# Nine block sums of a graph network on one Trainium2 core: gathered source rows and 32-wide one-hots in place of dense counts

## The chip, the cores and the metric

The kernel runs on one core of one Trainium2 chip. The metric is the device time of one execution in microseconds. The kernel before takes 1509.97 us (median of 3 runs, 1509.72 to 1510.40).

## What is computed

A graph of N = 6250 nodes has 206,250 edges (`src`, `dst`), sorted by `dst`. The input is normalised row by row and cut at zero; three layers follow, and the log-softmax of the last is added to the input:

```
def _mean_agg(x, src, dst, n):
    msg_sum = segment_sum(x[src], dst, num_segments=n)
    cnt = segment_sum(ones((src.shape[0], 1)), dst, num_segments=n)
    return msg_sum / maximum(cnt, 1.0)

def _sage_conv(x, src, dst, Wl, bl, Wr):
    return _mean_agg(x, src, dst, x.shape[0]) @ Wl.T + bl + x @ Wr.T

h = relu(layernorm(x))
h = relu(batch_norm(_sage_conv(h, ..., Wl0, bl0, Wr0)))   # 128 -> 256 features
h = relu(batch_norm(_sage_conv(h, ..., Wl1, bl1, Wr1)))   # 256 -> 256
h = _sage_conv(h, ..., Wl2, bl2, Wr2)                     # 256 -> 128
return x + log_softmax(h)
```

The edges are data: the program finds them on the chip. A flag says whether the quick way has found all of them; if not, a general and slow way (`general`) runs, which it does not do here.

## The kernel before

**Dense counts.** The destinations are cut into NB = 25 blocks of BD = 250 nodes, the sources into NA = 49 tiles of 128. For each block layer 0 builds a matrix C with one row per source and one column per destination; an entry is the number of edges between the two. A block's sum over its edges is then a product of features and C: 49 tiles, each feature matrix in two float16 parts (high and low), so 98 matmuls of 250 columns (`pe_agg`, L802). Layer 1 has 256 features and so 196 matmuls a block. Layer 2 first multiplies with its weights, which leaves 128 features and 98 matmuls. C is stored in DRAM (`C_dram`, 3.06 MB a block) while layer 0 runs and loaded again, half a block at a time, in layers 1 and 2 (`block_load`, L1160).

**Layer 0** runs over phases c = 0 to NB of NST = 13 steps each; step i of phase c counts ten of the 125 destination pairs of block c and adds a thirteenth of block c - 1's sum. Its parts in order of a block's way:
- ScalarE and VectorE find where the block's edges begin; GpSimd gathers a row of destinations (`pool_rows`, L331) and windows of 128 edges for each pair of destinations (`pool_windows`, L342). This is done for four blocks at once, in chores that `chores` puts at fixed steps. GpSimd, VectorE and TensorE turn the windows into a table (`pool_place`, L351 and L353; `dve_table`; `pe_turn`, L779).
- VectorE makes one-hots of source and position with `dve_hot` (L621), two operations for every two steps, in three buffers.
- TensorE multiplies them (`pe_cells`, L795, 10 matmuls of 98 columns a step) into four banks used in turn; ScalarE copies these as float16 into `ring` (L459).
- TensorE adds up the block before (`pe_agg`), VectorE divides by the degree (`dve_mean`, L630), TensorE multiplies with the weights (`pe_linear`, L810 and L813), ScalarE adds the bias, VectorE takes the statistics for the batch normalisation.

Layer 1 ends only when its statistics are in; so does layer 0.

**Layers 1 and 2** begin with a prelude: the features are normalised and turned (`pe_pair`, L1226) or multiplied (`pe_quad`, L1237), ScalarE and VectorE write the two parts, and TensorE adds up the first two blocks in between (their C is still in `ring`). Then come the other 23 blocks (`pe_layer1`, `pe_layer2`), each with the products of one finished block inside.

The order on each engine is the order of the Python code for it; engines meet at semaphores. Of the DMA queues, SP's carries loads, stores and C, GpSimd's the gathers only. GpSimd has nothing to do after layer 0's last table.

Steps and orders are set by these lines:

```
orders = [list(range(NB)), list(range(NB))[::-1], list(range(NB))]
...
for c in range(NB + 1):
    work = [(a, part) for a in range(NA) for part in range(2)]
    for i in range(NST):
        t = NST * c + i
        if c < NB:
            pe_cells(c, i)
        ...
        upto = len(work) * (i + 1) // NST
```

Of the kernel before, what the change touches and what calls it, by code (L numbers as in the profile page):

```python
# [6 lines left out]
F32 = mybir.dt.float32  # L7
F16 = mybir.dt.float16
# [5 lines left out]
P = 128  # L14
# [11 lines left out]
NTAB = 8  # L26

# [12 lines left out]
def gnn_program(nc, n_edges, x, pairs, dst_rows, samples, const_f, iota_h, WlT, WrT, vecs, out):  # L40
# [10 lines left out]
    assert N % BD == 0 and NW <= P and GPK * NW <= 512 and NT * P <= EP and NB >= 4  # L51
# [4 lines left out]

    batches = [(0, 1)]
    while batches[-1][1] < NB:
        batches.append((batches[-1][1], min(NB, batches[-1][1] + NBT)))
# [60 lines left out]
    def bank_before(t, h):  # L120

        t -= 2
        while t >= 0 and h >= banks_of(t):
            t -= 2
        return banks_upto(t) - banks_of(t) + h + 1 if t >= 0 else 0
# [3 lines left out]
    visit = {lc: v for v, lc in enumerate(visits)}  # L129
# [9 lines left out]
    nquad = -(-NA // 4)  # L139

    with ExitStack() as ctx:
# [49 lines left out]
        tot = sb("tot", [P, NB + 1])  # L191
# [19 lines left out]
        early = upper if NA * 128 >= need else sb("early", [P, need])  # L211
        win = early[:, 0:NBT * 256].bitcast(I32).rearrange("p (w n two) -> p w n two", w=NBT, two=2)
        wrk = early[:, NBT * 256:NBT * (256 + 3 * P)].rearrange("p (k n e) -> p k n e", k=3, e=P)
        hots = sb("hots", [P, NHOT - 1, HOT], F16)
        hot = [early[:, NBT * (256 + 3 * P):need].bitcast(F16)] + [hots[:, k, :] for k in range(NHOT - 1)]
        tab = sb("tab", [P, NTAB, 2, P], F16)
# [12 lines left out]
        def hot_pos(h):  # L229
            return hot[h % NHOT][:, 0:GPH * NW].rearrange("p (q x t) -> p q x t", x=NW, t=2)  # L230


# [7 lines left out]
        d_out = [sem(f"d_out{s}") for s in range(4)]  # L240

# [8 lines left out]
                             "v_z2", "v_dd", "v_fin", "v_own"))  # L250

        a_sample, a_inrow, a_degree, a_tab, a_cells, a_lnstd, a_relu, a_hi0, a_h0 = (
# [8 lines left out]
        n_set = GD + 1 + 5  # L261
# [10 lines left out]
        def lin_bank1(c):  # L272
            return [7, 2][c % 2]
# [23 lines left out]
        def sync_layer0():  # L297
# [14 lines left out]
            for c in range(NB + 1):  # L312
                if c >= 1:
                    rcb_load(c - 1)
# [4 lines left out]
                if c < NB:  # L319
                    sp.wait_ge(a_cells, banks_upto(NST * c + NST - 1))  # L320
                    sp.dma_start(C_dram[c, :, :], ring[:, c % 2, :]).then_inc(d_store[c % 2], 16)

# [37 lines left out]

        def pool_layer0():
# [7 lines left out]
            pool.memset(zeros_h[:, :], 0.0).then_inc(p_set, 1)  # L369
            pool_rows(0)  # L370
            pool_windows(0)
            pool_rows(1)
            pool_windows(1)
            for t in range(NST * NB):
# [7 lines left out]
                if t in ln_at and ln_at[t] in act_groups:  # L382
                    pool_lo(ln_at[t])

# [1170 lines left out]
```

## Time and profile before

| | |
|---|---|
| median of 3 runs | 1509.97 us |
| the profiled execution, its time | 1508.48 us |
| its span in the profile | 1506.7 us |
| TensorE matmul, busy | 1418.1 us, 94% |
| VectorE | 616.1 us, 41% |
| ScalarE | 544.1 us, 36% |
| GpSimd | 120.0 us, 8% |
| granted TensorE clock, mean | 0.993 |
| chain that ended last: TensorE, VectorE, ScalarE | 80%, 10%, 5% |
| layer 0 | from 0 to 550 us |
| layer 1 | 550 to 1177 us |
| layer 2 | 1177 us to the end |

The busy time of an engine is an average over three layers of different kinds, so what an edit is worth is read in its own layer. The chain that ended last is followed back from the last instruction: its shares tell which work the time hangs on. Times of the trace below count from the start of the span. Where a row of the timeline merges instructions (x4), its duration is that of all of them.

### The profile page before, as it was taken

To read this page: it belongs to the slowest core of one execution; us is meant where nothing else is said; L and a number is where in the kernel's file an instruction comes from. 1 tells how busy PE (TensorE), PEld (TensorE's weight loads), DVE (VectorE), ACT (ScalarE), POOL (GpSimd) and SP (SyncE) were. 2 spreads that over 40 slices of the span, in tenths; PEclk is the share of its full clock that TensorE was granted. 3 is DMA by queue.
4 is the path that set the end of the run, shared out by engine and by line. 5 is a ranking of instruction groups with operands and counts; after the bars stand their busy time and mean duration, and the time that the engine had idled before them with its cause. 6 is when DMAs were issued, how large, how long until landed. Compare 5 with 4: busy or idle time off the path is not lost.

```text
span 1506.7 us, 31846 instructions
## 1 busy us (share of the span) xinstructions
PE 1418.1 (94%) x14074; PEld 1280.7 (85%) x14074; DVE 616.1 (41%) x954; ACT 544.1 (36%) x1298; POOL 120.0 (8%) x81
## 2 busy tenths in 40 slices
PE   1499999999999989999999999999999899999997
PEld 1388898988898979899999999999999898888886
DVE  6998898989898943100000000000000222112212
ACT  4897979897878747100000000000000430000001
POOL 2323131313130000000000000000000000000000
PEclk9999999999999999999999999999999999999999
DMA  5244454545454422434343333334340358888882
GB/s 165 88 165 157 158 189 189 189 183 195 180 198 175 176 95 86 140 128 160 122 151 130 132 130 132 130 132 141 126 161 10 93 223 305 285 302 289 300 286 99
DMA packets 49914, 252.24 MB, mean 167 GB/s; under 512 B 7790, under 2 KB 31532, under 8 KB 34796
## 3 DMA queue, kind: packets, MB, share of 16 engines
q1 hardware_dynamic: 47372, 243.59, 45.4%
q0 software_dynamic: 2400, 6.56, 1.5%
q8 instruction: 114, 1.87, 0.5%
q14 instruction: 28, 0.23, 0.0%
HBM read 168.50 MB, written 81.62 MB: 166 GB/s over the span
## 4 chain that ended last, share of the span: by engine, by line
PE 80%; DVE 10%; ACT 5%; issue 3%; DMA 2%; POOL 1%; DVEq 0%; SPq 0%; POOLq 0%; ACTq 0%
PE bank L802 62%; PE bank L795 6%; DVE hots L621 5%; PE bank L810 4%; PE bank L813 4%; ACT ring L459 2%; DVE parts L621 2%; PE bank L1237 2%; PE bank L1439 1%; DMA parts<-in_pairs_dram,first_i 1%; ACT junk L412 1%; PE bank L1226 1%; POOL parts L351 0%; PE bank L1450 0%; ACT Z L436 0%
## 5 line engine op out<-in xcount | busy, mean ns | idle before, releaser
L802 PE MATMUL bank<-ring,parts 128*128 128x250 f16 x9800 | 1121.3, 270 | 1.3 <-DVE agm L630 1.1
L802 PEld LDWEIGHTS bank<-ring,parts 128*128 128x128 f16 x9800 | 937.6, 97 | 100.9 <-issue 1.6
L459 ACT CAST ring<-bank 128x490 f16<-128x490 f32 x625 | 322.8, 587 | 81.6 <-PE bank L795 79.1
L621 DVE TENSOR_TENSOR hots<-iotas,tab 128x2560 f16<-128x2560 f16 (+1 forms) x232 | 277.3, 1245 | 1.5 <-ACT tab L420 0.8
L1277 ACT ACTIVATE Z<-bank,vec 128x250 f32<-128x250 f32 x48 | 19.9, 466 | 529.5 <-PE bank L813 529.5
L630 DVE SCALAR_TENSOR_TENSOR agm<-bank,bnw,rcb 128x250 f32<-128x250 f32 x50 | 21.5, 473 | 375.4 <-PE bank L802 375.4
L795 PE MATMUL bank<-hots 128*128 128x98 f16 x2080 | 136.7, 212 | 33.3 <-DVE hots L621 30.8
L795 PEld LDWEIGHTS bank<-hots 128*128 128x128 f16 x2080 | 120.3, 99 | 47.1 <-DVE hots L621 36.4
L621 DVE TENSOR_TENSOR parts<-iotas,tab 128x2560 f16<-128x2560 f16 (+1 forms) x118 | 139.4, 1222 | 2.2 <-ACT tab L420 1.2
L1397 ACT ACTIVATE junk<-rows_i 128x128 f32<-128x128 f32 (+1 forms) x49 | 14.7, 301 | 253.0 <-DVE rows_i L1426 253.0
L693 DVE BATCH_NORM_STATS2 st<-Z 128x6 f32<-128x250 f32 x96 | 35.2, 408 | 152.8 <-ACT Z L1277 152.3
L630 DVE SCALAR_TENSOR_TENSOR agm<-bank,isp,rcb 128x250 f32<-128x250 f32 x25 | 11.9, 477 | 166.8 <-PE bank L802 166.8
L795 PE MATMUL bank<-parts 128*128 128x98 f16 x1045 | 69.0, 212 | 11.5 <-DVE parts L621 10.2
L795 PEld LDWEIGHTS bank<-parts 128*128 128x128 f16 x1045 | 60.2, 99 | 19.8 <-DVE parts L621 14.2
L810 PE MATMUL bank<-Z,wr 128*128 128x250 f32 x288 | 76.5, 374 | 0.0
L813 PE MATMUL bank<-agm,wl 128*128 128x250 f32 x288 | 76.5, 374 | 0.0
L813 PEld LDWEIGHTS bank<-agm,wl 128*128 128x128 f32 x288 | 54.8, 190 | 6.0
L331 POOL DMA_INDIRECT rows_i<-in_dst_rows_dram,row_i x25 | 41.5, 1661 | 191.7 <-DVE row_i L508 185.9
L1213 DVE TENSOR_TENSOR parts<-bank,parts 128x512 f16<-128x512 f32 (+2 forms) x38 | 25.6, 674 | 73.8 <-ACT parts L1207 73.8
L810 PEld LDWEIGHTS bank<-Z,wr 128*128 128x128 f32 x288 | 50.8, 190 | 4.6
L342 POOL DMA_INDIRECT parts<-in_pairs_dram,first_i x25 | 41.4, 1655 | 64.4 <-DVE first_i L515 58.9
L1191 ACT ACTIVATE Z<-Z,bnw 128x256 f32<-128x256 f32 (+2 forms) x76 | 45.9, 655 | 1.6 <-DVE bnw L1180 1.6
(118 smaller groups left out, 541.3 us busy)
## 6 DMA issues: line engine op xcount, KB each, us to landing
c_blocks<-ring SPq DMA_DIRECT2D x25, 3062.5 KB, 10.6
ring<-c_blocks SPq DMA_DIRECT2D x46, 1562.5 KB, 6.5
ring<-c_blocks SPq DMA_DIRECT2D x46, 1500.0 KB, 6.6
rcb<-rc_row SPq DMA_DIRECT2D x75, 125.0 KB, 7.7
Z<-in_x_dram SPq DMA_DIRECT2D x4, 768.0 KB, 6.7
out_dram<-rows_i SPq DMA_DIRECT2D x24, 128.0 KB, 5.3
smp_i<-in_samples_dram SPq DMA_DIRECT2D x1, 403.0 KB, 3.3
rows_i<-in_dst_rows_dram,row_i POOLq DMA_INDIRECT x25, 4.0
```

The costliest lines, as they stand in the source:

```text
L331: pool.indirect_dma_start(out=rows_i[:, k, :], out_offset=None, in_=dst_rows, in_offset=bass.IndirectOffsetOnAxis(ap=row_i[:, c:c + 1], ax ...
L342: pool.indirect_dma_start(out=win[:, k, :, :].rearrange("p n two -> p (n two)"), out_offset=None, in_=flat_pairs, in_offset=bass.IndirectO ...
L459: act.copy(blk[c % 2][:, :, d0:d0 + GD * GPK].rearrange("p a (g d) -> p a g d", d=GD), bank[(0, 1, 5, 6)[(2 * t + h) % 4]][:, 0:GPK * NW] ...
L621: ins = dve.tensor_tensor(o[:, 0:q, :, :], iota2[:, 0:w, :].unsqueeze(1).to_broadcast((P, q, w, 2)), place.unsqueeze(2).to_broadcast((P, q ...
L630: ins = dve.scalar_tensor_tensor(agm[:, v % 2, m, :], bank[b][:, 0:BD], scale if isinstance(scale, float) else scale[:, m:m + 1], rcb[:, v ...
L693: dve.bn_stats(st[:, m, b, :], Z[:, m, BD * b:BD * b + BD]).then_inc(v_stats, 1)
L795: ins = pe.matmul(b[:, o:o + NW], bs[:, q0 + g // 2, :, g % 2], ps[:, q0 + g // 2, :, g % 2], start=True, stop=True)
L802: return pe.matmul(bank[b][:, 0:BD], view[0:r, a, part, m * P:m * P + P], blk[c % 2][0:r, a, :], start=(a, part) == (0, 0), stop=(a, part) ...
L810: pe.matmul(bank[b][:, BD * m:BD * m + BD], wr[layer][:, k, m * P:m * P + P], Z[:, k, BD * c:BD * c + BD], start=(k == 0), stop=False)
L813: ins = pe.matmul(bank[b][:, BD * m:BD * m + BD], wl[layer][:, k, m * P:m * P + P], agm[:, v % 2, k, :], start=False, stop=(k == nk - 1))
L1191: act.activation(Z[:, k, c0:c0 + w], Z[:, k, c0:c0 + w], ACT.Relu, bias=bnw[:, layer, 5, k:k + 1], scale=bnw[:, layer, 4, k:k + 1]).then_i ...
L1237: ins = pe.matmul(bank[t % 3][0:r, P * (a - 4 * t):P * (a - 4 * t) + P], Z[:, k, P * a:P * a + r], wl[2][:, k, :], start=(k == 0), stop=(k ...
```

## The change

Of the 25 blocks, blocks 20 to 23 become "loose". Blocks 22 and 23 are no longer counted densely at all, blocks 20 and 21 are, as the first two of the new order `seq` of ND = 23 counted blocks. In layer 0 the sums of blocks 20, 22 and 23 are gathered, in layer 1 those of all four, in layer 2 those of 22 and 23: nine block sums.

Such a sum works on half blocks of 125 destinations ("windows"), cut into four spans of 31, 31, 31 and 32 destinations. Each span's edges stand in 9 (the last: 10) tiles of 128 edges. For a tile GpSimd gathers the 128 source rows from a table of the features in DRAM, both parts side by side (`pool_round`, an indirect DMA of 128 rows of 512 bytes in layers 0 and 2, of 1024 in layer 1). TensorE multiplies them with the tile's one-hot, 128 edges by 32 destinations (`pe_round`); the four spans write partitions 0, 32, 64 and 96 of one bank. A round is one tile of each span: 9 rounds a window, the last with a fifth tile, 37 gathers and 37 matmuls. There are 6, 8 and 4 windows, so 54, 72 and 36 rounds, and two buffers for a round's rows. Then VectorE divides, TensorE turns the sum (`pe_group_turn`), ScalarE writes it where the products read it (`act_gmean`), and the block's products follow (`lin_at`). Rounds are placed evenly between the dense steps by `place`: in layer 0 one every 4.26 steps from step 39 on, in layer 1 one every 12.2 tiles, in layer 2 one every 25.4 tiles.

New besides: the features go to DRAM as a table once a layer (`table_store`, on SP's queue: 3.2, 6.4 and 3.2 MB), and in layer 2 both its halves stand ahead of the first block loads; VectorE makes a one-hot of 1280 elements a window (`dve_group_hot`); one gather, a few small operations and 20 transposes early in layer 0 find the edges of the spans; two windows of layer 0 are only counted, against a column of ones. Counts in layer 0 now use three banks instead of four. Layer 0 has 24 phases instead of 26, and its first sum starts in phase 2, not 1.

```diff
+    loose = [NB - 5, NB - 4, NB - 3, NB - 2]
+    gathered = [[loose[0], loose[2], loose[3]], loose, loose[2:]]
+    seq = loose[0:2] + list(range(NB - 5)) + [NB - 1]
+    ND = len(seq)
+    wins = [[2 * loose.index(b) + h for b in gathered[layer] for h in range(2)] for layer in range(3)]
+    rounds = [[(n, k, t) for n, k in enumerate(wins[layer]) for t in range(RPG)] for layer in range(3)]
+    def tiles_of(t):
+        return [(t, j) for j in range(4)] + ([(t + 1, 3)] if t == RPG - 1 else [])
...
-    orders = [list(range(NB)), list(range(NB))[::-1], list(range(NB))]
+    orders = [list(range(1, ND)), list(range(2, ND))[::-1], list(range(2, ND - 1)) + [0, 1, ND - 1]]
...
+    begin = [3 * NST, 14, 24]
+    spans = [NST * (ND - 1), NA * (len(orders[1]) - 2) - 12, NA * (len(orders[2]) - 2) - 40]
+    for layer in range(3):
+        nh = len(rounds[layer]) + 2 + (len(only_counted) if layer == 0 else 0)
+        place.append([begin[layer] + (spans[layer] - begin[layer]) * h // nh for h in range(nh)])
...
+        for r in range(len(rounds[layer])):
+            take[layer].setdefault(at[r], []).append(r)
+    for r in range(len(rounds[0])):
+        fetch.setdefault(place[0][r - 2] if r >= 2 else begin[0] - 8, []).append(r)
...
+        def pool_round(layer, r):
+            n, k, t = rounds[layer][r]
+            if r >= 2:
+                pool.wait_ge(t_round, rbase[layer] + r - 1)
...
+            for i, (tile, j) in enumerate(tiles_of(t)):
+                o = 40 * k + 4 * tile + j
+                pool.indirect_dma_start(
+                    out=got[layer][:, 5 * (r % 2) + i, 0:rowf[layer]], out_offset=None, in_=tables[layer],
+                    in_offset=bass.IndirectOffsetOnAxis(ap=src_i[:, o:o + 1], axis=0)).then_inc(d_got[r % 2], 16)
...
-                                     bank[(0, 1, 5, 6)[(2 * t + h) % 4]][:, 0:GPK * NW]
+                                     bank[(0, 1, 5)[(n - 1) % 3]][:, 0:GPK * NW]
...
+        def pe_round(layer, r):
+            if t == 0:
+                pe_sums_free(layer, n)
+                pe.wait_ge(v_ghot, wbase[layer] + n + 1)
+            pe.wait_ge(d_got[r % 2], landed[layer, r])
+            g = ghot(layer, n)
+            for i, (tile, j) in enumerate(tiles_of(t)):
+                ins = pe.matmul(b[32 * j:32 * j + 32, 0:w], g[:, 2 * tile + j // 2, :, j % 2],
+                                got[layer][:, 5 * (r % 2) + i, 0:w], start=(tile == 0), stop=(tile == WT[j] - 1))
+            ins.then_inc(t_round, 1)
...
         def sync_layer2():
+            for a0, a1 in ((0, FULL // 2), (FULL // 2, NA)):
+                table_here(a_hi2, v_lo2, 4, a1)
+                table_store(2, small, a0, a1)
             for k in range(2):
                 block_load(2, 2, k)
                 block_load(2, 3, k)
```

GpSimd's queue in layer 0. Before, after the low parts of the features (L358), it holds row and window gathers and the place computations alone:

```order
L358 TENSOR_TENSOR parts<-Z,parts 128x4x128 x8
L358 TENSOR_TENSOR parts<-Z,parts 106x128
L331 DMA rows_i<-in_dst_rows_dram,row_i 128x256 x4
L342 DMA parts<-in_pairs_dram,first_i 128x256 x4
L351 TENSOR_SCALAR parts<-parts 128x512
L353 TENSOR_TENSOR parts<-parts 128x512
```

The same queue with the change, from the first place computation on (`got_f` holds the gathered rows, `src_i` their numbers, `table` is the features' table in DRAM; L491, L493, L471 and L482 are the L351, L353, L331 and L342 of before):

```order
L491 TENSOR_SCALAR parts<-parts 128x512
L493 TENSOR_TENSOR parts<-parts 128x512
L513 DMA got_f<-table,src_i 128x256 x29
L471 DMA rows_i<-in_dst_rows_dram,row_i 128x256 x4
L513 DMA got_f<-table,src_i 128x256 x12
L482 DMA parts<-in_pairs_dram,first_i 128x256 x4
L513 DMA got_f<-table,src_i 128x256 x9
L491 TENSOR_SCALAR parts<-parts 128x512
L493 TENSOR_TENSOR parts<-parts 128x512
L513 DMA got_f<-table,src_i 128x256 x28
```

Where 8 gathers stood for four blocks, some 50 more now stand between them, and the window gathers that VectorE waits for are behind them.

TensorE's queue in layer 0 with the change, two rounds apart (L1128 counts, L1135 adds up the dense block, L1188 is `pe_round`):

```order
L1128 MATMUL bank<-parts 128x98 x10
L1135 MATMUL bank<-ring,parts 128x250 x7
L1128 MATMUL bank<-parts 128x98 x10
L1135 MATMUL bank<-ring,parts 128x250 x8
L1188 MATMUL bank<-got_f,parts 32x257 x4
L1128 MATMUL bank<-hots 128x98 x10
L1135 MATMUL bank<-ring,parts 128x250 x7
```

Before, such rows are the pairs of count and sum alone; every fourth or fifth pair is now followed by a round, which waits for its landing with all that stands behind it.

SP's queue at the start of layer 2 with the change (L409 loads degrees, L460 is `table_store`, L1584 `block_load`):

```order
L409 DMA rcb<-rc_row 128x250 [waits v_mean] x2
L460 DMA table<-parts 128x24x256 [waits v_lo2,a_hi2] x2
L460 DMA table<-parts 106x256
L1584 DMA ring<-c_blocks 128x6250 [waits t_half] x2
L1584 DMA ring<-c_blocks 128x6000 [waits t_agg] x2
```

The three L460 rows are new and stand between the degrees and the block loads, which followed each other before.

## Rows read from the trace of the kernel before

**Rows 1.** Table by stretches: us, then busy us (instructions) per engine, clock, DMA share, GB/s.
```profile
111.00:540.00 429.00, 415.14 (x5152) 377.06 (x5149) 390.48 (x464) 350.19 (x804) 90.43 (x46) 1.00 0.49 182
...
640.00:1160.00 520.00, 520.00 (x4519) 469.92 (x4517) 34.43 (x86) 18.26 (x44) 0.00 (x0) 1.00 0.37 130
...
1240.00:1490.00 250.00, 250.00 (x2244) 224.37 (x2243) 51.18 (x132) 19.77 (x110) 0.00 (x0) 1.00 0.83 285
```

**Rows 2.** Chain of waits, its longest pieces: start us, us, what.
```profile
348.32 8.06 DMA parts<-in_pairs_dram,first_i
...
644.47 20.97 PE bank L802 x196
668.83 20.98 PE bank L802 x196
```

**Rows 3.** Timeline of TensorE in layer 0: start us, us, engine line op, operands, count.
```profile
129.08 0.63 PE L795 MATMUL bank<-hots 128*128 128x98 f16 x10
129.55 1.02 PE L802 MATMUL bank<-ring,parts 128*128 128x250 f16 x8
130.41 0.63 PE L795 MATMUL bank<-parts 128*128 128x98 f16 x10
```

**Rows 4.** Timeline of GpSimd, with the idle time before in brackets.
```profile
32.40 0.95 POOL L342 DMA_INDIRECT parts<-in_pairs_dram,first_i  x1 [0.30 <-issue]
...
74.36 1.08 POOL L358 TENSOR_TENSOR parts<-Z,parts 106x128 f16<-106x128 f32 x1 [2.74 <-ACT parts L439]
...
174.75 2.08 POOL L331 DMA_INDIRECT rows_i<-in_dst_rows_dram,row_i  x1 [38.86 <-DVE row_i L508]
...
179.54 2.19 POOL L331 DMA_INDIRECT rows_i<-in_dst_rows_dram,row_i  x1 [0.31 <-issue]
182.03 0.96 POOL L331 DMA_INDIRECT rows_i<-in_dst_rows_dram,row_i  x1 [0.30 <-issue]
192.00 2.00 POOL L342 DMA_INDIRECT parts<-in_pairs_dram,first_i  x1 [9.02 <-DVE first_i L515]
...
207.77 1.92 POOL L351 TENSOR_SCALAR parts<-parts 128x512 f32<-128x512 f32 x1 [7.53 <-DVE parts L530]
209.78 2.17 POOL L353 TENSOR_TENSOR parts<-parts 128x512 f32<-128x512 f32 x1
...
270.33 1.98 POOL L342 DMA_INDIRECT parts<-in_pairs_dram,first_i  x1 [9.02 <-DVE first_i L515]
```

**Rows 5.** Timeline of TensorE in layer 1's prelude: four transposes.
```profile
559.38 0.60 PE L1226 MATMUL bank<-cf,Z 128*128 128x128 f32 x4
```

**Rows 6.** Timeline of VectorE beside the gathers of 174.75 to 182.99 us.
```profile
174.42 2.58 DVE L621 TENSOR_TENSOR parts<-iotas,tab 128x2560 f16<-128x2560 f16 x2
176.92 5.07 DVE L621 TENSOR_TENSOR hots<-iotas,tab 128x2560 f16<-128x2560 f16 x4
181.90 0.73 DVE L693 BATCH_NORM_STATS2 st<-Z 128x6 f32<-128x250 f32 x2
182.55 0.92 DVE L621 TENSOR_TENSOR parts<-iotas,tab 128x768 f16<-128x768 f16 x2
```

**Rows 7.** Line L342: landings of four gathers at 28.6 to 32.4, then at 192.0 to 199.3.
```profile
DMA to landing us min/median/max: 2.6/2.7/3.1
...
DMA to landing us min/median/max: 3.4/5.9/7.9
```

**Rows 8.** Timeline of TensorE at layer 0's end.
```profile
533.50 4.99 PE L802 MATMUL bank<-ring,parts 128*128 128x250 f16 x45
...
554.70 0.53 PE L1226 MATMUL bank<-cf,Z 128*128 128x128 f32 x2 [5.05 <-ACT Z L1191]
```

**Rows 9.** Timelines of SP and TensorE at layer 2's start; the page's row of block stores.
```profile
1209.49 18.69 SPq L1160 DMA_DIRECT2D ring<-c_blocks  x4
...
1228.01 2.95 PE L802 MATMUL bank<-ring,parts 128*128 128x250 f16 x26 [0.45 <-DVE agm L630]
...
c_blocks<-ring SPq DMA_DIRECT2D x25, 3062.5 KB, 10.6
```

More of the change, by code:

```diff
@@ L139, in gnn_program @@
     nquad = -(-NA // 4)
+    begin = [3 * NST, 14, 24]
+    spans = [NST * (ND - 1), NA * (len(orders[1]) - 2) - 12, NA * (len(orders[2]) - 2) - 40]
+    place = []
+    for layer in range(3):
+        nh = len(rounds[layer]) + 2 + (len(only_counted) if layer == 0 else 0)
+        place.append([begin[layer] + (spans[layer] - begin[layer]) * h // nh for h in range(nh)])
+    near = max(0, min(3, (spans[0] - begin[0]) // len(place[0]) - 1))
+    take, fold, turn_at, lin_at, only_at, hot_at = ([{} for _ in range(3)] for _ in range(6))
@@ new lines, in gnn_program @@
+    for layer in range(3):
+        at = place[layer]
+        for r in range(len(rounds[layer])):
+            take[layer].setdefault(at[r], []).append(r)
+        for n, k in enumerate(wins[layer]):
+            e = RPG * (n + 1)
+            fold[layer].setdefault(at[e - 1] + near, []).append(n)
+            turn_at[layer].setdefault(at[e], []).append(n)
+            if n % 2:
+                lin_at[layer].setdefault(at[e + 1], []).append(gathered[layer][n // 2])
+            hot_at[layer].setdefault(at[max(0, e - RPG - 2)], []).append(n)
@@ new lines, in pe_sums_free @@
+        def pe_sums_free(layer, n):
+            if layer == 0 and n > len(wins[0]):
+                pe.wait_ge(v_gcnt, n)
+            elif gbase[layer] + n:
+                pe.wait_ge(v_gsum, gbase[layer] + n)
+        def pe_round(layer, r):
+            n, k, t = rounds[layer][r]
+            b = bank[sum_bank[layer]]
+            w = 257 if layer == 0 else rowf[layer]
+            if t == 0:
[7 more added lines that the diff above has]
+            ins.then_inc(t_round, 1)
@@ new lines, in pe_only @@
+        def pe_only(n):
+            i = len(wins[0]) + n
+            pe_sums_free(0, i)
+            pe.wait_ge(v_ghot, i + 1)
+            pe.wait_ge(p_set, n_set)
+            g = ghot(0, i)
+            for t in range(RPG):
+                for tile, j in tiles_of(t):
+                    ins = pe.matmul(bank[6][32 * j:32 * j + 32, 256:257], g[:, 2 * tile + j // 2, :, j % 2], ones_h[:, 0:1],
+                                    start=(tile == 0), stop=(tile == WT[j] - 1))
+            ins.then_inc(t_only, 1)
@@ new lines, in pe_group_turn @@
+        def pe_group_turn(layer, n):
+            pe.wait_ge(v_gsum, gbase[layer] + n + 1)
+            if gbase[layer] + n:
+                pe.wait_ge(a_gmean, sum(len(wins[k]) * 2 * (rowf[k] // 256) for k in range(layer)) + 2 * n * (rowf[layer] // 256))
+            for m in range(rowf[layer] // 256):
+                o = turned_at[layer] + P * m
+                ins = pe.transpose(bank[turned_bank[layer]][:, o:o + P], gsum[layer][:, P * m:P * m + P], ident)
+            ins.then_inc(t_gturn, 1)
```

742 lines of the change are left out of this document (554 added, 188 removed).

## The prediction, before the changed kernel was run

> **What bounds the kernel now.** I read the table by stretches first, then the chain of waits, then the timelines of each engine. In layer 1 TensorE is busy for the whole 520.00 us of the stretch and VectorE for 34.43; in layer 2 the same, with the DMA engines at 0.83 of their time [rows 1]. The chain shows layer 1 as TensorE alone: 196 matmuls of a dense block in 20.97 us, 107 ns each, block after block 24.36 us apart, the rest being the products with the weights [rows 2]. So whatever leaves TensorE there is gained in full. Layer 0 is different. In its 429 us TensorE is busy 415, VectorE 390, ScalarE 350 [rows 1], and the chain passes through GpSimd's gathers of the edge windows, which take 8.06 us to land [rows 2]. A step (one of 13 of a block) costs TensorE 0.47 us of counting and 0.86 us or less of block sum [rows 3]; the real pace is read from two window gathers that lie four blocks, 52 steps, apart: 270.33 - 192.00 = 78.3 us, 1.51 us a step and 19.6 us a block [rows 4].
>
> **What goes.** Layer 1 loses four dense blocks: 4 x 20.97 = 83.9 us [rows 2]. Layer 2 loses two of 98 matmuls: 196 x 0.107 = 21.0 us. Layer 0 loses two of its 26 block phases (each 19.6 us, so 39 us) and the sums of one more block. The products with the weights all stay.
>
> **What comes on TensorE.** A half block needs 37 matmuls of 32 result rows, in four column strips, the longest strip ten deep. Layer 1 has 8 such windows of 512 columns, 296 matmuls; a matmul of 512 columns by the 107 ns of 250 is 219 ns [rows 2]. If the four strips run side by side, that is 80 x 0.219 = 17.5 us; if one after the other, 64.8. The trace of before has no matmul in a strip. I take 22, near the lower end, since the four write different partitions of one bank and no data of one feeds another. Layer 2: 148 matmuls of 256 columns, 4.4 to 16.3 us, taken as 5.5. The turns add 16 transposes in layer 1 and 4 in layer 2, at 0.15 us [rows 5]: 2.4 and 0.6 us.
>
> For strips only a page has a price. The Trainium skill (TensorE: Matmul & The Clock Gate, Part 3, Measured speedup vs the span model) gives 2.38 times for three column strips; by that, an estimate, the two layers would pay 27 + 7 us and the sum would be 6 us higher. No row here shows it.
>
> **What comes on GpSimd, and this decides.** 222 + 296 + 148 gathers of 128 rows. Their price is in the trace twice over. Where VectorE runs short work only, a gather, as the one at 32.40, is 0.95 us busy and 0.30 us behind the last: one in 1.26 us. In layer 0 they start 2.43 us apart on average, (182.03 - 174.75) / 3, and last 2.08 to 2.19 us [rows 4]. The difference is what VectorE does: one-hots back to back, each an operation with two SBUF inputs, 2.5 us a pair; and the fourth issue, again 0.96 us, fell just where a batch statistic ran instead [rows 6]. Each gather waits through two one-hots. Landing grows from 2.7 to 5.9 us at the median [rows 7]. So I price a gather at 1.26 us of VectorE's free time or 2.49 us of its one-hot time.
>
> A page goes further. The Trainium skill (SBUF — State Buffer, Who interferes with whom, and the warning on DMAs from GpSimd ahead of it) has an exclusive lock that blocks the other engine for a whole instruction, with a DMA going from about 620 to 3100 ns beside a copy. Five times 0.95 us would be an estimate of 4.75 us a gather, and the sum some 70 us higher; the rows agree with the lock, not with the factor.
>
> Layer 0, per round of 4.11 gathers, 54 rounds over the steps 31 to 264. GpSimd also has 36 of its old gathers there (0.67 a round) and five place computations of 1.92 + 2.17 us [rows 4] (0.38 us a round). VectorE's one-hot time is 6 pairs of 2.49 and one of 0.87 us a block [rows 6], 15.8 us, 18 blocks, so 5.3 us a round. In those 5.3 us GpSimd does 2.1 of its 4.78 gathers, the other 2.65 need 3.34 us free: the round takes 5.3 + 3.34 + 0.38 = 9.0 us. TensorE's own work between two takes is 4.26 steps x 1.51 = 6.4 us. GpSimd is slower, so TensorE stands at each take until the rows land, in order, with the counting and the dense sum behind it; VectorE then stops when its three one-hot buffers are full, which is where the free time comes from. The landing time itself is hidden, as two buffers of rows alternate. The first gather waits for the table in DRAM: the last low parts are made by 75.4 us [rows 4], and its 3.2 MB take like a block's store some 10.6 us [rows 9]; so 88 us. 88 + 54 x 9.0 = 574, + 3 to land = 577. Then 34 steps at 1.51 us and a last phase without counting, as before from about 535 to 549.7 [rows 8], 14 us: layer 0 ends at 643 instead of 549.7, **93 us later**. The 54 rounds' own matmuls (6 to 24 us) and the removed sums lie under GpSimd's time and count nothing; without that cover both would show. Three banks instead of four for the counts cost nothing for the same reason: ScalarE, which empties them, has 350 of 429 us busy and TensorE's stops give it more.
>
> Layers 1 and 2 are not held by GpSimd: one-hots are gone, a round is 4.11 x 1.26 = 5.2 us, and TensorE has 12.2 steps of 0.43 us plus products between takes, 6.2 us or more. At the starts something is late. In layer 1 the table's last quarter leaves SP only when the last parts are made; behind two half loads, then some 5.3 us to write (half a block's store), 5 to issue round 0, 3 to land, against some 13 us until the first take: 3 us. In layer 2 SP now issues both table halves, which wait for the last low parts, ahead of the first block loads. The four half loads took 18.69 us from 1209.49, 4.7 each, and TensorE wanted the first at 1228.01 [rows 9]. Started at about 1225 behind 1.6 MB, the first half lands near 1235 and the second near 1244: 11 us of waiting in all, between 0 if the loads catch up and 20.
>
> **The sum**, on the profiled execution's 1508.5 us: layer 0 +93; layer 1 -83.9 + 22 + 2.4 + 3 = -56.5; layer 2 -21.0 + 5.5 + 0.6 + 11 = -4. That is 1541; the median of the runs lies 1.5 above the profiled one, so **1542 us**.
>
> **Rivals.**
> A. The gathers keep the quiet 1.26 us in layer 0 too. Then GpSimd needs 4.78 x 1.26 + 0.38 = 6.4 us a round, just TensorE's own pace, and layer 0 gains: -39, about -5 for the third block's sum, +16 for matmuls of rounds no longer covered, -28 in all. Total 1510 - 28 - 60 = **1422 us**. For it: the quickest landing in layer 0's burst is 3.4 us after its issue, near the quiet 2.7 [rows 7]. Against: every burst in layer 0 has its first three issues at 2.0 to 2.2 us. 8%. A page points this way: the Trainium skill (DMA: Bandwidth & Descriptors, Anatomy of one DMA) calls the generation of descriptors small and most of the 2 us a receipt. The trace contradicts it, with 0.95 us on GpSimd for each even when quiet.
> B. The other sign by the same mechanism, only weaker: layer 0 loses less than the others gain. The other layers give 60.5 us; so the rounds must end 32 us sooner, a round of 8.4 us, which is a gather at 2.04 us in one-hot time. At 1.7 us a round takes 7.8, layer 0 is 26 us longer, and with strips fully side by side and no start waits (-75) the total is **1461 us**. For it: the 2.43 is from bursts of four, never from a stream. 10%.
> C. The strips run one after the other: +43 and +11 in layers 1 and 2, none in layer 0: **1596 us**. 12%.
> D. GpSimd's order hurts too: windows of the next blocks now stand behind gathers, VectorE waits for them before it makes one-hots, and gathers wait for TensorE's rounds. Each of five batches losing 8 us more, as one window's landing [rows 2]: **1582 us**. 15%.
> The forecast itself, contention at 2.2 to 2.8 us and strips mostly parallel: 55%.
>
> **Numbers.** Low end: a gather at 2.04 us (the point of B) with strips fully parallel and no start waits, 1495, and a little of B; high end: C with a round at 9.2 us, 1605. I give 1485 to 1605, which leaves out A, most of B and what lies beyond C and D together. A change of 0.2% (3 us) is about what can be measured. Faster over 0.2%: A and B and the low tail, 0.20; within: 0.02; slower: 0.78.
>
> **What would show it.** GpSimd gathers of about 2 us in layer 0 and 0.95 us later; TensorE's wait before the 257-column matmuls, released by the landing, near 2.5 us x 54; VectorE idle about a third between 100 and 580 us; layer 0's last matmul near 643 us. Layer 1 blocks still 24.4 us plus four rounds; four 512-column matmuls in about 0.3 us, not 0.88. Wrong if issues in layer 0 are 1.26 us apart, or TensorE's waits there are on one-hots, or the granted clock falls in the gaps and layer 0 becomes longer than GpSimd's time.

## The result and the profile after

The changed kernel takes **1622.24 us** (median of 4 runs, 1616.38 to 1636.87) against 1510.18 for the kernel before (median of 4, 1509.72 to 1511.29): ratio 1.0755, 95% interval 1.0684 to 1.0827. It is slower, as forecast, but by 112 us where 32 were forecast, and outside the range. The profiled execution took 1621.26 us, with a span of 1619.3.

The layers end where TensorE waits five microseconds for the normalised features. From the timeline of TensorE after the change, the first rows of layers 1 and 2, and the first row behind layer 2's prelude:

```profile
697.29 1.11 PE L1650 MATMUL bank<-cf,Z 128*128 128x128 f32 x4 [5.05 <-ACT Z L1615]
...
1284.27 1.01 PE L1661 MATMUL bank<-wl,Z 128*128 128x128 f32 x3 [5.24 <-ACT Z L1615]
...
1340.60 1.64 PE L1135 MATMUL bank<-ring,parts 128*128 128x250 f16 x7 [11.27 <-DMA ring<-c_blocks]
```

A layer's end is the start of that wait: 697.29 - 5.05 = 692.2, and 1279.0. Before, by the same rule, 549.7 [rows 8] and 1177.3.

| | before | after | difference | forecast |
|---|---|---|---|---|
| layer 0 | 549.7 | 692.2 | +142.5 | +93 |
| layer 1 | 627.6 | 586.8 | -40.8 | -56.5 |
| layer 2 to the end | 329.4 | 340.3 | +10.9 | -4 |

The table by stretches, the same stretches as [rows 1]:

```profile
111.00:540.00 429.00, 333.13 (x3611) 276.67 (x3608) 270.47 (x329) 247.04 (x565) 292.84 (x221) 0.88 0.45 151
640.00:1160.00 520.00, 505.94 (x4532) 433.12 (x4530) 96.05 (x211) 90.22 (x206) 233.30 (x244) 0.99 0.56 191
1240.00:1490.00 250.00, 230.83 (x2011) 200.82 (x2010) 47.96 (x109) 40.93 (x110) 93.73 (x99) 0.96 0.67 229
```

In layer 0 no engine is full. TensorE gets 3611 matmuls done in 429 us where it had 5152; by the busy time of one before (415.14 / 5152) they are 291 us of work. They took 333, and 33 of these 42 us lie in stretches at the lower clock: the granted clock fell to 0.88, with 18 stretches between 100 and 640 us, 123 us in all, at 1.2 GHz, where before there is one of 3.4 us, behind the layer's end. The other 96 us are waits. GpSimd is busy 293 of 429 us. Its gathers, and what they waited for, from the groups of instructions between 100 and 640 us:

```profile
L513 POOL DMA_INDIRECT got_f<-table,src_i x222 | 297.9, 1342 | 154.7 <-PE bank L1188 94.3 <-issue 57.2 <-remote 3.1
```

1.34 us on average, and a wait of 94 us for TensorE's rounds: GpSimd waits for TensorE far more than TensorE for it. TensorE's waits between 111 and 640 us, and ScalarE's (engine, tile and line, released by: us, times, longest). "Issue" stands where no wait is found that ended just then, "remote" where a signal came at a moment at which no recorded instruction ended:

```profile
PE bank L1128 <- ACT ring L632: 43.2, 40, 4.5
PE bank L1128 <- issue: 29.7, 18, 4.8
PE bank L1188 <- DMA got_f<-table,src_i: 17.1, 5, 9.7
PE bank L1128 <- DVE hots L830: 15.5, 4, 8.7
...
ACT ring L632 <- PE bank L1128: 154.9, 169, 5.7
ACT ring L632 <- remote: 45.6, 23, 5.2
```

TensorE's waits for gathered rows to land, the takes (L1188), cost 17 us, not 54 times 2.5. The counting (L1128) waits for ScalarE's copies, and ScalarE's copies (L632) wait for the counting. One such place, in the timeline of TensorE, then of ScalarE, VectorE and GpSimd:

```profile
218.22 0.40 PE L1128 MATMUL bank<-hots 128*128 128x98 f16 x5
221.66 0.59 PE L1128 MATMUL bank<-hots 128*128 128x98 f16 x5 [3.05 <-issue]
222.05 1.86 PE L1135 MATMUL bank<-ring,parts 128*128 128x250 f16 x8
223.71 0.61 PE L1128 MATMUL bank<-hots 128*128 128x98 f16 x5
228.85 0.59 PE L1128 MATMUL bank<-hots 128*128 128x98 f16 x5 [4.52 <-ACT ring L632]
```

```profile
222.49 0.57 ACT L632 CAST ring<-bank 128x490 f16<-128x490 f32 x1 [0.89 <-PE bank L1128]
228.22 1.04 ACT L632 CAST ring<-bank 128x490 f16<-128x490 f32 x2 [5.16 <-remote]
...
228.39 2.58 DVE L830 TENSOR_TENSOR hots<-iotas,tab 128x2560 f16<-128x2560 f16 x2 [10.01 <-remote]
...
221.66 0.95 POOL L513 DMA_INDIRECT got_f<-table,src_i  x1 [0.30 <-issue]
...
225.44 0.96 POOL L513 DMA_INDIRECT got_f<-table,src_i  x1 [0.30 <-issue]
```

Every copy empties the five matmuls of one bank, and all 575 copies and 2875 counting matmuls are in the trace, so they can be paired by number. The copy at 228.22 belongs to the matmuls at 218.22. ScalarE had been idle for 5 us, VectorE for 10, both on the same signal of TensorE, which the trace's semaphore record has at 228.20, 9.6 us behind the end of those matmuls; the next two banks' signals follow at 228.27 and 228.40, though their matmuls started 2 us apart. **TensorE's signals arrive late, in a bunch, while GpSimd issues gathers 1.26 us apart.** Counted over the layer from 100 us on: 69 of 514 copies begin more than 0.5 us after both their matmuls (by the trace's ends) and ScalarE's earlier work are over, 105 us together. Before it is 0 of 560. The record of signals says the same without any pairing: of the 626 of TensorE between 100 and 690 us, 131 come more than 0.5 us behind the end of the last matmul that could have sent them, before none of 682; those of ScalarE, VectorE and GpSimd are all within 0.02 us. The ends of matmuls are modelled in such a trace, so a late signal cannot be told from a matmul that ended late. With three banks between the two engines, TensorE then waits too. That reading needed experiments.

### The profile page after: what moved, and what is told of

Read it like the earlier page. It is cut to its first block, busy times and chain, and to the rows that moved or that the text cites. A ratio compares the mean times of both kernels' runs of the same rounds, so it can differ in the third digit from the quotient of the medians.

```text
span 1619.3 us, 31087 instructions
## 1 busy us (share of the span) xinstructions
PE 1398.3 (86%) x13334; PEld 1188.7 (73%) x13334; DVE 615.7 (38%) x1013; ACT 537.2 (33%) x1285; POOL 805.7 (50%) x746
## 4 chain that ended last, share of the span: by engine, by line
PE 70%; issue 7%; POOL 6%; ACT 5%; DMA 5%; DVE 5%; another core or an unknown queue 2%; SPq 0%; DVEq 0%; ACTq 0%; POOLq 0%
PE bank L1135 49%; PE bank L1128 7%; POOL got_f L513 4%; PE bank L1150 3%; PE bank L1153 3%; PE bank L1188 3%; ACT ring L632 3%; DMA got_f<-table,src_i 2%; DVE hots L830 2%; PE bank L1661 1%; DMA hots<-table,src_i 1%; PE bank L1935 1%; POOL hots L513 1%; PE bank L1650 1%
## 5 line engine op out<-in xcount | busy, mean ns | idle before, releaser
L1135 PE MATMUL bank<-ring,parts 128*128 128x250 f16 (+1 forms) x8526 | 1023.9, 274 | 14.9 <-DMA ring<-c_blocks 11.3
L1135 PEld LDWEIGHTS bank<-ring,parts 128*128 128x128 f16 (+1 forms) x8526 | 820.6, 99 | 133.0 <-issue 22.8
L513 POOL DMA_INDIRECT hots<-table,src_i x444 | 425.2, 958 | 528.3 <-DMA table<-parts 236.4
L632 ACT CAST ring<-bank 128x490 f16<-128x490 f32 x575 | 302.6, 579 | 242.4 <-PE bank L1128 175.8
L513 POOL DMA_INDIRECT got_f<-table,src_i x222 | 297.9, 1342 | 154.7 <-PE bank L1188 94.3
L830 DVE TENSOR_TENSOR hots<-iotas,tab 128x2560 f16<-128x2560 f16 (+1 forms) x214 | 253.1, 1230 | 52.3 <-PE bank L1128 31.3
L1128 PE MATMUL bank<-hots 128*128 128x98 f16 x1915 | 144.0, 223 | 94.3 <-ACT ring L632 42.2
L1128 PEld LDWEIGHTS bank<-hots 128*128 128x128 f16 x1915 | 117.8, 105 | 118.3 <-DVE hots L830 42.8
L830 DVE TENSOR_TENSOR parts<-iotas,tab 128x2560 f16<-128x2560 f16 (+1 forms) x108 | 128.0, 1227 | 23.2 <-PE bank L1128 21.6
L1128 PE MATMUL bank<-parts 128*128 128x98 f16 x960 | 72.2, 222 | 38.3 <-ACT ring L632 17.7
L1128 PEld LDWEIGHTS bank<-parts 128*128 128x128 f16 x960 | 58.8, 105 | 51.0 <-ACT ring L632 21.0
L1153 PE MATMUL bank<-agm,wl 128*128 128x250 f32 x256 | 69.3, 378 | 0.0
L1188 PE MATMUL bank<-hots 128*32 128x512 f16 (+1 forms) x444 | 41.7, 356 | 5.5 <-DMA hots<-table,src_i 5.5
```

The costliest lines, as they stand in the source:

```text
L513: pool.indirect_dma_start(out=got[layer][:, 5 * (r % 2) + i, 0:rowf[layer]], out_offset=None, in_=tables[layer], in_offset=bass.IndirectOf ...
L632: act.copy(blk[c % 2][:, :, d0:d0 + GD * GPK].rearrange("p a (g d) -> p a g d", d=GD), bank[(0, 1, 5)[(n - 1) % 3]][:, 0:GPK * NW] .rearra ...
L830: ins = dve.tensor_tensor(o[:, 0:q, :, :], iota2[:, 0:w, :].unsqueeze(1).to_broadcast((P, q, w, 2)), place.unsqueeze(2).to_broadcast((P, q ...
L1128: ins = pe.matmul(b[:, o:o + NW], bs[:, q0 + g // 2, :, g % 2], ps[:, q0 + g // 2, :, g % 2], start=True, stop=True)
L1135: return pe.matmul(bank[b][:, 0:BD], view[0:r, a, part, m * P:m * P + P], blk[c % 2][0:r, a, :], start=(a, part) == (0, 0), stop=(a, part) ...
L1153: ins = pe.matmul(bank[b][:, BD * m:BD * m + BD], wl[layer][:, k, m * P:m * P + P], mean[:, k, :], start=False, stop=(k == nk - 1))
```

## The experiments

My theories from this trace: **G**, the gathers that GpSimd issues hold up the others; **S**, the strip matmuls of the rounds do; **B**, three count banks instead of four. Layer ends below are read as above; "late copies" are those just counted (how many, and us together).

| run | layer 0 ends | layer 1 | layer 2 | time, us | late copies, us |
|---|---|---|---|---|---|
| before | 549.7 | 627.6 | 329.4 | 1510.2 | 0 |
| changed | 692.2 | 586.8 | 340.3 | 1622.2 | 69, 105 |
| no_gathers_l0 | 548.6 | 587.6 | 339.8 | 1477.8 | 2, 2 |
| three_banks_before | 554.6 | 629.1 | 329.4 | 1514.9 | 0 |
| whole_array_rounds | 693.3 | 615.3 | 344.6 | 1655.1 | 65, 99 |
| idle_gathers_before | 676.1 | 628.8 | 329.1 | 1636.0 | 57, 93 |
| idle_loads_sp | 556.7 | 627.9 | 329.4 | 1515.9 | 0 |
| idle_loads_pool | 566.4 | 629.3 | 329.4 | 1527.1 | 4, 5 |
| idle_gathers_spread | 682.5 | 628.3 | 329.8 | 1642.3 | 61, 98 |
| idle_gathers_32rows | 685.3 | 629.1 | 330.0 | 1646.1 | 62, 117 |
| busy_gpsimd | 603.5 | 628.7 | 329.4 | 1563.4 | 6, 7 |
| idle_gathers_56 | 567.4 | 628.6 | 329.1 | 1527.2 | 0 |
| idle_gathers_layer1 | 550.9 | 627.6 | 329.2 | 1509.5 | 0 |
| loads_first_layer2 | 697.7 | 587.5 | 348.4 | 1635.3 | 62, 102 |
| dense_layer0 | 563.5 | 588.6 | 392.1 | 1547.5 | 3, 4 |
| dense_layer0_order | 564.1 | 588.6 | 343.6 | 1497.1 | 3, 4 |
| gathers_layer1_only | 559.8 | 587.9 | 327.7 | 1477.5 | 0 |

The last three rows are medians of four or five runs, the other experiments single runs (kernel before beside them: 1507.8 to 1509.2).

### The gathers taken out, and put alone into the kernel before

```diff
 # no_gathers_l0, in pool_round and pe_round
+            if layer == 0:
+                if r == 0:
+                    pool.wait_ge(d_table[0], 32)
+                return
...
-            pe.wait_ge(d_got[r % 2], landed[layer, r])
+            if layer:
+                pe.wait_ge(d_got[r % 2], landed[layer, r])
```

> The changed kernel without the 222 gathers of layer 0: its 54 rounds of strip matmuls stay, on rows that hold ones throughout, and wait for nothing that lands. (Left out: the gathered features of three block sums, so their values are not the reference's.) Layer 0 ended at 692 us with the gathers. Theory G, the gathers hold up the counting, TensorE's reports of finished counts arriving up to 5 us late while GpSimd issues them: layer 0 ends at 525 to 550 us (549.7 before, less 39 for two phases, plus 54 rounds of some 0.4 us), the total 1455 to 1485 us, no report later than 0.1 us, the clock over 0.98. Theory S, the strip matmuls hold up TensorE by themselves: layer 0 still ends beyond 660 us and the total stays over 1590. Theory B, three count banks instead of four: the same as S.

```diff
 # idle_gathers_before, in pool_layer0 of the kernel before, at 56 steps
+                    pool.wait_ge(t_cells, banks_upto(t))
...
+                    for k in range(4):
+                        pool.indirect_dma_start(
+                            out=idle_rows[:, 4 * (r % 2) + k, :], out_offset=None, in_=x,
+                            in_offset=bass.IndirectOffsetOnAxis(ap=row_i[:, k:k + 1], axis=0)).then_inc(d_idle[r % 2], 16)
```

> The kernel before with 56 groups of four extra gathers on GpSimd in layer 0, of 128 rows of 512 bytes of the input into a buffer that nobody reads, each group issued once TensorE has counted a certain step, one group per 4.25 steps from step 39 on. TensorE, VectorE, ScalarE and their waits are untouched. Theory G: layer 0 ends at 600 to 690 us instead of 549.7 although no engine waits for the gathers, and TensorE's reports arrive late. Theories S and B: layer 0 ends at 550 to 558 us (GpSimd's row and window gathers a little later), total under 1518. If the forecast's price holds, the extra gathers are issued 2 to 2.5 us apart.

Both came out as G says. Without the gathers layer 0 ends at 548.6: they cost 143.6 us, 0.65 each. Of these TensorE's waits are 96 us (from 20 to 116) and the longer time of the same matmuls 47 (from 428 to 475, at a granted clock of 0.90 and not 1.00). Put alone into the kernel before, 224 of them cost 126.4 us, 0.56 each, though nothing that the kernel computes waits for them; three banks, strips and takes are all absent. Here the waits are 76 us more and the matmuls' time 50. They lasted 1.42 us on average and started 1.57 us apart at the median, where I had priced 2 to 2.5. The worst place, in the timelines of TensorE and of ScalarE in that run:

```profile
276.68 0.30 PE L810 MATMUL bank<-hots 128*128 128x98 f16 x3 [0.48 <-issue]
278.12 0.37 PE L817 MATMUL bank<-ring,parts 128*128 128x250 f16 x1 [1.15 <-issue]
278.84 0.37 PE L817 MATMUL bank<-ring,parts 128*128 128x250 f16 x1 [0.35 <-issue]
280.27 0.37 PE L817 MATMUL bank<-ring,parts 128*128 128x250 f16 x1 [1.06 <-issue]
281.67 0.57 PE L817 MATMUL bank<-ring,parts 128*128 128x250 f16 x2 [1.03 <-issue]
283.10 0.37 PE L817 MATMUL bank<-ring,parts 128*128 128x250 f16 x1 [0.86 <-issue]
...
285.26 0.57 ACT L474 CAST ring<-bank 128x490 f16<-128x490 f32 x1 [7.94 <-remote]
```

Here TensorE not only signals late. It crawls: a matmul or a weight load every 0.71 us, with no wait to name ("issue"), for 10 us, while eight gathers are issued 1.25 us apart. In this run 46 such steps of over 0.5 us stand between 111 and 540 us, in the kernel before none. In the changed kernel there are 2: there the late signals and the waits behind them do the harm, and the crawl is hardly seen.

A third part is GpSimd's order, rival D of the prediction. VectorE waits 41.5 us for landed windows and place computations, which stand behind the idle gathers, against 6.5 before. Of that little reaches TensorE: it waits 18 us for one-hots and not 10.

### Banks and strips

```diff
 # three_banks_before, in pe_cells and act_layer0 of the kernel before
-                b = bank[(0, 1, 5, 6)[(2 * t + h) % 4]]
...
+                b = bank[(0, 1, 5)[no % 3]]
...
 # whole_array_rounds, in pe_round
-                ins = pe.matmul(b[32 * j:32 * j + 32, 0:w], g[:, 2 * tile + j // 2, :, j % 2],
...
+                ins = pe.matmul(b[:, 0:w], ones_h[:, :],
...
```

> The kernel before with three count banks (0, 1, 5) used in turn in place of four, nothing else. Theory B, fewer banks tie TensorE to ScalarE: layer 0 ends beyond 580 us instead of 549.7, total over 1540. Theories G and S: at most 5 us more, total 1508 to 1515.

> The changed kernel with all gathers, but every matmul of a round multiplies with a 128 x 128 matrix of ones into all 128 partitions, instead of a 32 wide one-hot into a strip. (Left out: the selection of edges, so nine block sums are wrong, and the flag is set without its comparison.) Theory S: layer 0 falls to 530 to 560 us and reports of finished counts are on time. Theory G: layer 0 stays at 680 to 705 us with reports up to 5 us late. In layer 1 the four matmuls of 512 columns of a round then cost 4 x 0.219 = 0.88 us each round; if strips ran side by side (0.25 us) the layer grows from 587 by 72 x 0.6 = 43 us to 630, if strips were served one after the other it stays at 587.

B costs 4.9 us. S falls: with no strips layer 0 is as long as with them. The second run also prices the strips. Layer 1 is 28.5 us longer with whole matmuls; these are 296 x 0.219 = 64.8 us by [rows 2], so the strips cost 36.3. In layer 2, with 256 columns, it is 4.3 of 148 x 0.107 x 256 / 250 = 16.2, so 11.9; 4.3 us is little between two single traces. The timeline of a round in layer 1 of the changed kernel looks cheaper than that:

```profile
797.91 0.40 PE L1188 MATMUL bank<-hots 128*32 128x512 f16 x4
798.25 1.99 PE L1135 MATMUL bank<-ring,parts 128*128 128x250 f16 x17
```

The next matmul starts 0.34 us after the round's first, but by the layer's length a round costs 36.3 / 72 = 0.50.

### What about a gather does it

```diff
 # idle_loads_sp, on SP's queue                # idle_loads_pool, on GpSimd's
+  sp.dma_start(idle_rows[...], x[...])        +  pool.dma_start(idle_rows[...], x[...])
 # idle_gathers_spread: one per step, not four per 4.25     # idle_gathers_56: one per 4.25 steps
 # idle_gathers_32rows: out=idle_rows[0:32, ...], ap=row_i[0:32, ...]
 # busy_gpsimd: pool.tensor_scalar(idle_rows[:, 2:4, :], idle_rows[:, 0:2, :], 1.0, 0.0, ...) x4
```

> The kernel before with the same 224 extra transfers of 128 rows of 512 bytes of the input, 56 groups of four released by the same counted steps, but as plain loads on SP's hardware queue; GpSimd does nothing new. The idle gathers on GpSimd cost 126 us (layer 0 ended at 676). Theory T, the traffic into SBUF and its completions hold TensorE's reports up: layer 0 ends beyond 640 us here too. Theory I, it is GpSimd's issuing of DMAs that does: layer 0 ends at 550 to 560, total 1510 to 1520, TensorE's reports on time.

> The same extra transfers as plain loads of fixed rows from GpSimd's queue, no list of row numbers. Theory I in its narrow form (only gathers by row number, whose descriptors GpSimd works out from the list): layer 0 ends at 550 to 560. In its wide form (any DMA that GpSimd issues): beyond 640. Theory T: beyond 640.

The same bytes cost 7 us from SP's queue and 17 from GpSimd's, so it isn't the bytes (the 17 lie between what the narrow and the wide form of theory I allowed; that the loads read fixed rows in order and the gathers rows by number was not tested apart). The groups of GpSimd's extra instructions, idle_gathers_before first, then idle_loads_pool:

```profile
L394 POOL DMA_INDIRECT idle_rows<-in_x_dram,row_i x224 | 318.0, 1420 | 112.7 <-issue 55.5 <-PE bank L810 46.4 <-remote 5.5
```

```profile
L394 POOL DMA_DIRECT2D idle_rows<-in_x_dram x224 | 120.2, 550 | 155.3 <-PE bank L809 153.8 <-issue 1.3
```

A plain load takes 0.55 us each time, beside the same one-hots.

> The kernel before with the same 224 idle gathers on GpSimd, but one released by each of the 224 steps from 39 on, instead of four by every 4.25 steps. If the harm comes from gathers issued back to back (each late report in the traces lies beside two or more gathers of 0.95 us, 0.30 apart), spreading them ends most of it: layer 0 at 560 to 600 us, reports less than 2 us late. If each gather costs its share wherever it stands, layer 0 ends at 660 to 690 as with the groups.

> The kernel before with the 224 idle gathers on GpSimd cut to 32 rows each (partitions 0 to 31), all else as with 128 rows, which cost 126 us. If the harm goes with the rows (descriptors) that GpSimd writes: a quarter, 31 us, layer 0 ends at 575 to 590. If it goes with the gathers, whatever their size: layer 0 ends at 650 to 680.

> The kernel before with 224 extra GpSimd operations in place of the idle gathers, four per 4.25 steps as there, each a multiply-add of 128 x 256 float32 from one spare buffer to another (about the 0.95 us of a gather), no DMA. If GpSimd being busy beside VectorE is what does the harm (SBUF access), layer 0 ends beyond 620 us as with the gathers. If it is the issuing of gathers, layer 0 ends at 555 to 580 us (VectorE's one-hots a little longer) and TensorE's reports are on time.

> The kernel before with one idle gather of 128 rows per 4.25 steps in layer 0, 56 in place of 224. If the price goes with the number (126 us / 224 = 0.56 us each): 31 us, layer 0 ends at 575 to 590. If only dense streams of gathers do harm: layer 0 ends below 560.

The spread run cost 132.8 us, 0.59 each, but it did not spread the gathers: 197 of its 224 start right behind another instruction of GpSimd, 1.57 us apart at the median, as in the groups (198, 1.57 us). So it says nothing of gathers that stand apart. Fewer rows do not help (135.6 us for a quarter of the rows): my guess of a price by row missed. A GpSimd that is as busy with arithmetic costs 53.8 us, more than I allowed, but with few late signals (6 late copies): TensorE waits there 31.5 us for one-hots in 25 places. Two causes stand in the trace and were not tested apart. VectorE's one-hots of layer 0 take 22 us longer in all (those of 1960 elements 1.28 us and not 1.17), and VectorE waits 19 us for landings and place computations behind the extra work in GpSimd's order, where it was 6.5. In the runs with gathers the one-hots are not longer (1.17 to 1.18 us).

With 56 gathers the cost is 17.7 us, 0.32 each, between what the two theories allowed, and no copy is late. Nor is a single gather quick there. The group of these gathers, by GpSimd's lines:

```profile
L393 POOL DMA_INDIRECT idle_rows<-in_x_dram,row_i x56 | 120.6, 2154 | 150.0 <-PE bank L809 146.9 <-issue 2.9
```

That is 2.15 us on average beside VectorE's one-hots, which is the length that the prediction read. In a stream most take 0.95, since VectorE stands still too. The late signals came only with a stream of gathers; most of the 17.7 us here are TensorE's waits, 7 us more for one-hots and 7 more for ScalarE.

```diff
 # idle_gathers_layer1: the same gathers in layer 1 of the kernel before, ten behind each block
```

> The kernel before with 230 idle gathers on GpSimd in layer 1 instead of layer 0, ten after each dense block. There no engine waits for TensorE within a block. If the harm is that TensorE's reports come late to engines it waits for: layer 1 stays at 627 to 630 us, total 1508 to 1513. If gathers slow TensorE itself (0.56 us each): 1630 or more.

230 gathers, ten in a row 1.26 us apart, cost nothing there (627.6 as before), and between 640 and 1160 us TensorE has none of the steps of over 0.5 us. In these kernels the gathers were dearest where TensorE, ScalarE and VectorE hand work to each other every half microsecond. Why TensorE itself crawls in layer 0 and not here is not shown.

### Layer 2, and a version that is faster than both

```diff
 # loads_first_layer2, in sync_layer2; begin = [3 * NST, 14, 110]
+            for k, (a0, a1) in enumerate(((0, FULL // 2), (FULL // 2, NA))):
+                block_load(2, 2, k)
+                block_load(2, 3, k)
+                table_here(a_hi2, v_lo2, 4, a1)
+                table_store(2, small, a0, a1)
```

> The changed kernel with one difference, in layer 2: SP issues the half loads of the first two blocks ahead of each half of the table, and rounds start at tile 110 instead of 24. If the 11.3 us wait for the block was made by the table's stores ahead of it, layer 2 takes 318 to 330 us instead of 340.3 (11.3 less, and up to 7 more from the slow clock behind the gap). If the loads are late for another reason, it stays at 338 to 342.

The 11 us wait goes, as expected, but in this one run the layer is 8 us longer; its total lies among the changed kernel's four (1616 to 1637). The rounds also start later here, at tile 110, and so stand closer. SP's waits in layer 2 of this run, then of the changed kernel:

```profile
SPq L1584 <- remote: 63.1, 9, 10.2
```

```profile
SPq L1584 <- remote: 9.0, 1, 9.0
```

L1584 is the block load, which waits for TensorE's signal that a half of the ring is free. Nine such waits, up to 10.2 us long, ended with a signal at which no matmul's end is recorded. Blocks took up to 18 us, where most take 12.2 with rounds and 11.6 before. That the one made the other is not shown: no wait of TensorE for a block load is in this trace. Its waits in the layer sum to 25 us in both, though the 11 us wait is gone. The order of the queue was not the only thing that gathers do to layer 2, and mending it did not pay.

```diff
 # dense_layer0: loose = [0, 1, 2, 3], gathered = [[], loose, loose[2:]], seq = list(range(NB)), loads first
 # dense_layer0_order: loose = [NB - 6, NB - 5, NB - 4, NB - 3]
 # gathers_layer1_only: the same, gathered = [[], loose, []], layer 2 as before
...
+    orders = [list(range(ND)), [ND - 1, ND - 2] + list(range(ND - 6))[::-1], list(range(ND))]
```

> The change kept in layers 1 and 2 alone: layer 0 counts and sums all 25 blocks densely again, with four count banks and no gathers of features (blocks 0 to 3 are the loose ones, their eight windows are only counted), and in layer 2 SP issues the half loads of the first two blocks ahead of each half of the table, rounds starting at tile 110 instead of 24. Theory G: layer 0 ends at 550 to 556 us; layer 1 lasts 587 as in the changed kernel (627.6 before); layer 2, without the 11 us wait for the block and the slow clock behind it, 318 to 330 (329.4 before, 340.3 with the change). Sum 1457 to 1475 us, faster than before by 35 to 53. If layer 1's gain needed something of layer 0's change, or the loads are not what layer 2 waited for, the total is over 1480.

> The version with a dense layer 0 again, with blocks 19 to 22 loose instead of 0 to 3 and the counted blocks in natural order, so that the final log-softmax pieces, which need the lowest blocks first, do not pile up at the end (the version with blocks 0 to 3 spent 62 us after its last block, 1481.6 to 1544). Layer 0 563 us as there, layer 1 588, layer 2 315 to 325: total 1466 to 1478 us, ratio 0.972 to 0.980 to the kernel before. If layer 2's length was not made by that pile, the total stays above 1500.

> The version with the dense layer 0 and natural order, with gathers in layer 1 alone: layer 2 is the dense one of the kernel before. Layer 0 563 us, layer 1 589, layer 2 330: total 1481 to 1486 us, ratio 0.981 to 0.985 to the kernel before, and faster than the version with gathers in layers 1 and 2 (1497). If layer 2's gathers paid for themselves after all: 1497 or more.

dense_layer0 was a miss (ratio 1.0264, 1.0247 to 1.0281): layer 0 ends 7.5 us later than I allowed, layer 1 is as expected, but the gathered blocks were the lowest ones, finished last, and the final pieces need the lowest blocks first. In its timeline of TensorE, from 1481 us on, one piece after the other:

```profile
1485.94 0.66 PE L1941 MATMUL bank<-cf,Z 128*128 128x128 f32 x2 [1.74 <-DVE rows_i L1892]
1488.34 0.66 PE L1941 MATMUL bank<-cf,Z 128*128 128x128 f32 x2 [1.74 <-DVE rows_i L1892]
```

With other blocks that is gone (1497.05 us, ratio 0.992, 0.9898 to 0.9941), but layer 2 still takes 343.6, 14 more than with dense blocks only, and the ratio misses the 0.972 to 0.980 that I expected. **Gathers in layer 1 alone** give 1477.54 us, ratio 0.9806 (0.9791 to 0.9822): faster than the kernel before by 30 us and than the changed one by 145. Layer 0 pays 10 us there for finding the edges and counting eight windows, layer 1 gains 40.

## Why the prediction was wrong

- **Layer 0: GpSimd's pace, +93.** This step failed. The price of a gather in one-hot time (2.49 us, round 9.0 us) holds for gathers one at a time (2.15 us in idle_gathers_56), but not in the stream: VectorE stood still too, and 122 of 222 took 0.95. The rounds did come 9.5 us apart ((622.7 - 121) / 53), but that agreement is an accident: GpSimd waited 94 us for TensorE. What held the layer was 143.6 us that the gathers take from the other three engines: 96 us of TensorE's waits, by late signals and the waits that follow, and 47 us of longer matmuls, mostly by the lower clock between them. The forecast had the sentence "the granted clock falls in the gaps and layer 0 becomes longer than GpSimd's time" as what would prove it wrong, and gave it no price.
- **The takes, 2.5 us x 54**: 17 us in all. The gathers started 1.55 us apart at the median, nearer to the 1.26 that was named as a sign of being wrong than to 2.49.
- **"The 54 rounds' matmuls and the removed sums lie under GpSimd's time".** Without that cover they show: two phases less are -39.2, three banks +4.9 (I had nothing), and 548.6 leaves +33.2 for rounds, turns and the finding of edges, less the third block's sum.
- **Layer 1, -56.5**: right in kind. -83.9 stays; the strips cost 36.3 and not 22; with 2.4 for turns and 3.1 waited for the first rows (forecast 3) that is -42.1, measured -40.8. The strips lie between the bounds of 17.5 and 64.8, nearer the lower one, but 14 us above what I took.
- **Layer 2, -4**: the 11 us at the start came as forecast (11.3). The strips cost 11.9, not 5.5, and behind the gap the clock is at 1.2 GHz for 13.7 us, by an estimate 7 lost. -21 + 11.9 + 0.6 + 11.3 + 7 = +9.8, measured +10.9.
- **Rival A** is instructive: its condition held in part (122 of the 222 gathers at 0.95 us, 37 still over 1.9) and its gain did not come. The rule named beside it (the Trainium skill, DMA: Bandwidth & Descriptors, Anatomy of one DMA) calls the generation of descriptors small; here a gather did the same harm with 32 rows as with 128. In **B** the -75 should be -80 by its own terms, which leaves the range as it is. **C** was true by about a third: the strips cost 21 us more than I took, of its 54. **D** came about, but small: in the changed kernel VectorE waits 40 us for windows and place computations and not 6.5, and TensorE 17 us for one-hots and not 10.
- **The pages.** For three strips the Trainium skill (TensorE: Matmul & The Clock Gate, Part 3, Measured speedup vs the span model) has 2.38 times. Four strips brought 64.8 / 36.3 = 1.8 here at 512 columns and 16.2 / 11.9 = 1.4 at 256. By the Trainium skill (SBUF — State Buffer, Who interferes with whom, and ahead of it A bandwidth-pool intuition that's wrong, which has the figures) I had estimated 4.75 us a gather and a sum of 1612. Its factor is that of a copy beside a DMA. The 222 gathers took 1.34 on average, so the sum lies near the measured time by luck.

## What to carry to other kernels

GpSimd's idle time is not free for gathers by row number where other engines exchange signals every microsecond: price a stream of them as dense as this one at 0.6 us of everybody's time each, until a run says less. The same gathers beside a long run of matmuls of one engine cost nothing in layer 1 here, so that is the place to try them first. And put such a load alone into the kernel before, read by nobody, ahead of building what needs it: one run of that kind would have given 126 of the 142 us.

## What was not expected of the hardware

- Beside a stream of GpSimd's gathers TensorE's signals came up to 9.6 us late in the changed kernel, and in the kernel before with idle gathers its stream also slowed to one instruction in 0.71 us. Signals of ScalarE, VectorE and GpSimd itself are on time in the same traces (0.01 us behind the end). By what path is open: the number of rows, the bytes and GpSimd's being busy are excluded as its only cause, plain loads from the same queue do it hardly.
- 32 rows cost as much as 128.
- 56 gathers scattered among VectorE's one-hots took 2.15 us each on average, 224 plain loads from the same queue beside the same one-hots 0.55.
- The four matmuls of a round are recorded within 0.4 us, as if side by side, but strips bring 1.4 to 1.8 times, not four.
- Holds of TensorE of 2 to 11 us were followed by 3.4 to 13.7 us at 1.2 GHz. In layer 0 of the changed kernel the stretches at that clock added 33 us to 96 us of waits (111 to 540 us).
